# The weighing of a step issued ahead of the next step's third score, in a fused attention kernel

## What is computed

```
x = x + _L0_attn_ref(_layernorm(x, axis=-1), ...)
x = x + _L0_ffn_ref(_layernorm(x, axis=-1), ...)
x = x + _L1_attn_ref(_layernorm(x, axis=-1), ...)
x = x + _L1_ffn_ref(_layernorm(x, axis=-1), ...)

scores = jnp.einsum('bhtd,bhsd->bhts', q, k) / scale
attn = jax.nn.softmax(scores, axis=-1)
out = jnp.einsum('bhts,bhsd->bhtd', attn, v)
out = out.transpose(0, 2, 1, 3).reshape(Bb, Tt, C)
return jnp.einsum('btc,oc->bto', out, Wo) + bo
```

## Time and profile before

| | |
|---|---|
| median of 3 runs | 2943.95 us |
| lowest and highest | 2941.54, 2946.24 us |
| the profiled execution's own time | 2944.78 us |
| its span, first to last instruction | 2943.5 us |
| TensorE, VectorE, ScalarE busy | 79%, 70%, 50% of the span |
| first and last exponential of the first layer's attention | 866.4, 1608.8 us |
| of the second layer's | 1797.3, 2540.1 us |

### The profile page before, as it was taken

One profiled execution on the slowest core, in us unless ns is written; L12 is line 12 of the kernel. 1 busy time (PEld: TensorE's weight loads), 2 busy tenths in 40 slices (PEclk: granted clock), 3 DMA queues, 4 the chain that ended last, 5 costly groups with the idle time before them and its releaser, 6 DMA issues. The chain is left out here.

```text
span 2943.5 us, 37846 instructions
## 1 busy us (share of the span) xinstructions
PE 2323.2 (79%) x13096; PEld 1285.4 (44%) x13096; DVE 2053.8 (70%) x3485; ACT 1479.5 (50%) x2898; POOL 503.9 (17%) x410
## 2 busy tenths in 40 slices
PE   6888856933399999999998559999999999639920
PEld 5667745721144444344443224444444443239920
DVE  6667657635578888888881667888888887266635
ACT  4443320411117777777777104777777777513510
POOL 2223301756400000000000320000000000005644
PEclk9999965966659999999999757999999999857965
DMA  4000010343300000000000320000000000201211
GB/s 165 0 0 0 0 35 18 99 69 114 115 25 12 23 17 19 24 12 24 12 1 5 125 90 12 24 20 16 23 12 24 12 12 1 79 22 50 69 49 50
DMA packets 65302, 109.11 MB, mean 37 GB/s; under 512 B 11120, under 2 KB 45040, under 8 KB 64880
## 3 DMA queue, kind: packets, MB, share of 16 engines
q1 hardware_dynamic: 56176, 88.60, 8.9%
q0 software_dynamic: 8960, 18.37, 2.9%
HBM read 64.46 MB, written 41.94 MB: 36 GB/s over the span
## 5 line engine op out<-in xcount | busy, mean ns | idle before, releaser
L1043 DVE TENSOR_REDUCE mx<-psum 128x1 f32<-128x1024 f32 x1024 | 1216.0, 1220 | 273.4 <-PE psum L923 273.4
L1023 ACT ACTIVATE p<-psum 128x512 f32<-128x512 f32 x2048 | 1086.5, 599 | 493.1 <-PE psum L959 486.4
L959 PE MATMUL psum<-qs,ks 64*128 64x512 f32 x2048 | 838.4, 453 | 13.5 <-ACT p L1023 13.0
L923 PE MATMUL psum<-ks,qs 64*128 64x512 f32 x2048 | 689.4, 461 | 81.7 <-DVE mx L1043 44.1
L923 PEld LDWEIGHTS psum<-ks,qs 64*128 64x128 f32 x2048 | 312.3, 195 | 565.8 <-DVE mx L1043 425.2
L969 PE MATMUL psum<-p,v_ext 128*32 128x512 f32 x4096 | 547.8, 607 | 1.4 <-ACT p L1023 1.4
L959 PEld LDWEIGHTS psum<-qs,ks 64*128 64x128 f32 x2048 | 368.6, 185 | 242.3 <-ACT p L1023 212.3
L157 PE MATMUL psum<-ident,xn 128*128 128x128 f32 x160 | 44.3, 454 | 264.1 <-DVE xn L125 219.8
L575 ACT ACTIVATE hid<-psum,stage 128x128 f32<-128x128 f32 x448 | 132.5, 367 | 181.4 <-PE psum L545 181.4
L519 POOL DMA_INDIRECT x_in<-n_rows,token_of x152 | 167.1, 1100 | 251.0 <-POOLq L78 183.7
L649 POOL COPY n_all<-xn 128x1024 f32 x4 | 4.2, 1040 | 883.4 <-DVE xn L132 883.4
(11 more groups left out here) (171 smaller groups left out, 2378.2 us busy)
## 6 DMA issues: line engine op xcount, KB each, us to landing
qs<-qk_parts SPq DMA_DIRECT2D x128, 100.0 KB
ks<-qk_parts SPq DMA_DIRECT2D x128, 100.0 KB
answers<-y_out SPq DMA_DIRECT2D x152, 64.0 KB, 1.5
qk_parts<-qh SPq DMA_DIRECT2D x16, 512.0 KB, 4.5
qk_parts<-kh SPq DMA_DIRECT2D x16, 512.0 KB, 4.4
ew<-in_moe SPq DMA_DIRECT2D x1, 5136.0 KB, 18.1
ew<-in_moe SPq DMA_DIRECT2D x1, 4624.0 KB, 14.0
n_rows<-xn SPq DMA_DIRECT2D x8, 512.0 KB, 3.2
```

The source lines that it names most:

```text
L923: last = pe.matmul(psum[:, bank + h, :], a["qs"][r, g % NKF, i * P:(i + 1) * P], a["ks"][r, g % NKF, j % KM, h * HALF:(h + 1) * HALF], sta ...
L959: pe.matmul(psum[:, S_BANK + n % NS, :], a["ks"][r, g % NKF, j % KM, i * P:(i + 1) * P], a["qs"][r, g % NKF, h * HALF:(h + 1) * HALF], sta ...
L1023: act.activation(a["p"][:, n % NP, :], psum[:, S_BANK + n % NS, :], ACT.Exp, scale=DH ** -0.5)\
L1043: dve.tensor_reduce(a["mx"][:, g % 2, c:c + 1], psum[:, bank:bank + 2, :].rearrange("p a d -> p (a d)"), AX.X, ALU.max).then_inc(used, 1)
```

## The change

Only the order of two calls in TensorE's loop is changed:

```diff
                 score(s, 1)
                 if one:
                     fill(one, (1,))
-                score(s, 2)
                 if s:
                     weigh(s - 1)
+                score(s, 2)
                 if two:
                     fill(two, (0,))
                 score(s, 3)
```

## The result

The changed kernel takes 2971.18 us, the median of 4 runs (2965.39 to 2975.12); the kernel before took 2944.26 in the runs beside it (2941.54 to 2946.24). The ratio is 1.0091, with a 95% interval of 1.0072 to 1.0109: 27 us slower. The profiled execution took 2975.12, with a span of 2973.8.

What follows compares the result with a forecast made beforehand. It took a ring through TensorE and ScalarE, 2.61 us a step, to bound the kernel. Per group, +0.56 regular steps, +0.66 copy-and-turn blocks, -0.16 maxima's turn gave +34 us on 2944.8: 2978.5 us, range 2953 to 3004.

Steps and rivals of the forecast that it cites:

- The ring: TensorE and ScalarE wait on each other each step; score 2's 0.42 leaves, an exponential's 0.49 enters: 2.68 us for 2.61.
- A regular step: Step without copy or turn, 8 of a group's 16: 2.68 us for 2.61, +0.07 a step, +0.56 a group.
- The copy: copy_out between exp 2 and exp 3, nearly hidden before, adds 0.49: its step becomes 3.17 us for 2.71, all in the ring.
- The turning steps: Two steps around a turn of output or maxima: 6.39 us together, for 6.52 and 6.55, score 2 leaving the reduction's road.
- upper bound of 6.62: Two turning steps together, if the weighing keeps its 0.55 behind the maximum's second half: 6.62 us instead of 6.39.
- The sum: A 16-step group goes from 45.9 to 46.95 us, +1.06; two layers of 16 groups make +34 us.
- Rival A: Packing wins: TensorE's issue sets the step, which falls to VectorE's 2.35; 67 us faster, 2878 us; 7%.
- B: The copy stays hidden in ScalarE's idle time: +0.08 a group, some 3 us, 2947 us; 6%.
- D: A wash: the exponential follows score 2 by 0.47, not 0.54; the group changes by -0.06, 2943 us; 5%.
- Rival C: More than the sum: weighing follows pairs by 0.55, 15 + 22 us more, 3016 us, or the granted clock falls; 12%.

Runs made afterwards that it cites:

- a_more2: Changed kernel plus a small unused ScalarE copy behind exp 2 of every step: 3059.21 us, 88 over the change.
- a_more1: Changed kernel plus the same small unused ScalarE copy, but behind exp 1 of every step: 2971.59 us.
- b_more2: Kernel before the change plus a small unused ScalarE copy behind exp 2 of every step: 2945.02 us, ratio 1.0007.
- a_copy1: Changed kernel with copy_out between exp 1 and exp 2 instead of between exp 2 and exp 3: 2946.07 us, ratio to the kernel before 1.0013.
- a_unpaired: Changed kernel with score 3 directly behind score 2 and both halves of the second maximum behind them: 2975.62 us, ratio to the kernel before 1.0109.
- w_end_wait: Changed kernel with weighing at step end ahead of the turns, copy_out behind exp 3, exp 0's second wait moved to exp 2: 2860.78 us, ratio to before 0.9711.

## Why the prediction held

The forecast was 2978.5 in a range of 2953 to 3004, and 2971.2 was measured: right in sign and mechanism, 7 us too high (34 us forecast, 27 measured). By its steps:

- **The ring.** It said that score 2's 0.42 leaves and an exponential's 0.49 comes in. The timeline shows just this, `a_more2`, `a_more1` and `b_more2` show that exp 2 and exp 3 are both in it, and that in the old order the place between them was free.
- **A regular step:** 2.68 forecast, 2.67 measured; +0.06 and not +0.07. The interval from weighing to score to exponential is as it was before; two exponentials take 1.08 here and not 1.09.
- **The copy:** 3.17 forecast for its step, 3.16 measured. `a_copy1` puts a price on it: 25 us for the 62 copies, 0.40 each.
- **The turning steps:** copy and turn 9.56 forecast, 9.57 measured; the maxima's turn 6.39, measured 6.40. The weighing follows the last matmul by 0.32 (1047.94 to 1048.26) and does not keep its 0.55, so the upper bound of 6.62 did not come up.
- **The sum.** The forecast's groups of 46.95 us are 46.9 by the measured steps (8 x 2.67 + 2 x 9.57 + 6.40). With 45.9 before, 1.0 x 32 = 32 us; what the attention's first to last exponential gained in the profiled execution is 28.5 us (the line's own view: 867.9 to 2570.1 us, before 866.4 to 2540.1), of 30.3 in the span.
- **What the sum left out.** The trace, read from group to group, shows the rest. 20 groups inside the layers grew by 0.93 each (45.94 to 46.87). The six with an output projection, for which the prediction put nothing, grew by 0.44 only, which is 3 us less in all; why was not followed further. The last group but one of each layer grew by 1.2, and the last by 3.3, of which 1.6 is one step at the lower clock (4.46 where the same kind of step took 2.90 before it); the first of each layer shrank by 0.7 and 1.1, because the lower clock (0.50) lasted 7.2 and 8.1 us into the attentions before and 1.4 and 1.3 after. The two effects of the clock are luck: the stretch of low clock at the start is between 1.3 and 8.1 us long in the traces of either order. In `b_more2`, the old order, the first group with 7.4 us of it took 2.0 us longer than the one with 1.4. Here they nearly cancel, 3.1 us more against 3.7 less. Without them the attentions grew by 29: 30 for 32 groups at 0.93, 3 less for the projections, 2 more for the last steps of each layer, against the forecast's 34.
- **Rival A** had TensorE's issue as the bound. TensorE saved 66 us of busy time and the kernel slowed down; it is ruled out. **B** (the copy hidden) is ruled out by `a_copy1`. **D** (a wash) is not what happened, though it describes `a_copy1`: without the copy, +0.06 in the regular steps and -0.11 to -0.15 in the turning pairs nearly cancel.
- **Rival C** came true in one corner. The granted clock is 0.50 in the first microseconds of each attention, as before the change, and then 1.00 for as long as there are maxima. In the last 20 steps of a layer, which have none, it fell in some executions. The busy time by stretch of the changed kernel shows 0.91 near the end of either layer, where the kernel before shows 1.00, and `a_unpaired` shows 0.50 in one layer. The changed kernel, busy time by stretch, the clock in the column behind POOL:

```profile
1600.00:1620.00 20.00, 16.80 (x88) 5.36 (x86) 0.55 (x2) 14.16 (x28) 0.00 (x0) 0.91 0.00 0
```

The kernel before, in its last steps:

```profile
1580.00:1600.00 20.00, 17.09 (x98) 5.42 (x97) 0.55 (x2) 16.67 (x33) 0.00 (x0) 1.00 0.00 0
```

`a_unpaired`, a stretch near the end of its first layer:

```profile
1600.00:1620.00 20.00, 18.51 (x60) 4.43 (x57) 0.00 (x0) 10.86 (x21) 0.00 (x0) 0.50 0.00 0
```

ScalarE's timeline there (its exponential is L1022 in this kernel):

```profile
1596.19 2.08 ACT L1022 ACTIVATE p<-psum 128x512 f32<-128x512 f32 x4 [1.99 <-PE psum L959]
1600.26 2.08 ACT L1022 ACTIVATE p<-psum 128x512 f32<-128x512 f32 x4 [1.99 <-PE psum L959]
```

And `w_end_wait`, without maxima too:

```profile
1520.00:1540.00 20.00, 16.35 (x92) 5.02 (x90) 0.83 (x3) 15.54 (x31) 0.00 (x0) 1.00 0.00 1
```

At the lower level (1.2 GHz) such a step takes 4.07 us. The last steps of the first layer of `a_unpaired` took 13.5 us longer than those of its second, where the clock stayed at 1.00. The profiled execution took 14.5 us more than the median of its five runs; its mean clock is 0.863, that of the others 0.868 to 0.870. So the fall differs from one execution to the next. That may be why the changed kernel's runs spread over 10 us where those of the kernel before spread over 5; no run here tried to hold the clock up in those steps. The Trainium skill ("TensorE: Matmul & The Clock Gate", A second HAM failure mode: psum-queue depth-cycling) tells of a kernel in which short idle times between matmul groups made the clock swing. This trace agrees only in the steps without maxima, where TensorE is busy 84% of a window, for 85 to 88% before the change. The busy share does not tell the cases apart: `w_end_wait` is busy 82% there and stays at 1.00.

## What to carry to other kernels

Where two engines hand work back and forth, find the ring: follow one step in order of time, add the intervals until they close on the step's length, and ask of an edit only which intervals leave the ring and which come in. An instruction that leaves TensorE's part can put one of ScalarE's in, and a side job that was free in one order (the copy of 0.5 us) is paid in full in the other, so side jobs have to be placed again after each change of order. The best place for the weighing was one where it waits for nothing and covers another engine's latency: behind the step's last score, ahead of the turns, the weighing brought 2% instead of costing 0.9%.

## What was not expected

- A second semaphore wait costs ScalarE some 0.05 us even where it was met long before, if the exponential starts on a score that has just come: exp 0 starts 0.59 behind its score with two waits and 0.54 with one. Behind another exponential it costs nothing. In a ring of 2.6 us, 512 times, that was 27 us (0.9%), as `w_end_wait` shows.
- One operation of ScalarE of 128x512 occupies it for 0.49 us from start to start, though its record lasts 0.60; whoever waits for its result pays the 0.60.
- Inside the attentions TensorE's granted clock fell in steps without maxima alone, and not in every execution: one layer of `a_unpaired` ran through them at 0.50, the other at 1.00.
- The weighing that waits for the copy and the exponentials starts 0.14 to 0.15 behind the copy where the copy ends last, and 0.05 behind the exponential where the copy ended long before.
